# A GraphSAGE layer with batch norm on one core: second-stage loads behind the last gathers, four tiles kept for a late turn, sums before squares

## The chip, the cores and the metric

One core of a Trainium2 chip. The metric is the device time of one execution in microseconds. TensorE is PE in the profile, VectorE DVE, ScalarE ACT, GpSimd POOL and SyncE SP.

## The reference

`x` is 50000 x 512 float32. The edges are 12500 random pairs in both directions and a loop at each node, sorted by target (75000 in all). Cut to what matters:

```python
summed = segment_sum(x[src], dst, n)
cnt    = segment_sum(ones, dst, n)
aggr   = summed / maximum(cnt, 1.0)[:, None]
h      = aggr @ W_l.T + b_l + x @ W_r.T
mu     = mean(h, axis=0);  var = mean(square(h - mu), axis=0)
h_norm = (h - mu) * rsqrt(var + 1e-5) * gamma + beta
out    = layernorm(x + relu(h_norm), axis=-1)
```

## The kernel before, in words

**Stage one** makes `h` in HBM (`h_scratch`) and its column sums. It writes `h = x @ (W_l + W_r).T + (aggr - x) @ W_l.T`. The first product is made for all rows; the second is zero for a node whose only edge is its loop, so it is made only for the others, the "slots".

- *Products.* 78 groups of 640 rows (five tiles of 128) and a last one of 80 rows, 391 tiles. Each float32 operand is split in a high and a low part, and a tile is twelve matmuls into `pd` (`product`, L506, L524 to L526). SP loads `raw`, ScalarE rounds it to `x_hi` (`x_high`, L722), VectorE makes `x_lo` (`x_low`, L1042; four operations to a group, placed behind the group before's tile number 2). ScalarE copies `pd` to `h_out` (`copy_h`, L730), and behind a group's tiles 1 and 2 makes two `x_hi` pieces of the next group each. SP stores the group.
- *Slots.* 78 pairs of 128 slots. For a pair, VectorE makes one-hot tables and indices (`indices`, L1055), GpSimd gathers five blocks of rows (`gather`, L1356: `xe`, then `xn` and `xf` for both halves h), VectorE begins the difference (`begin`, L1074), TensorE adds the extras (`spread_extras`, L606), VectorE ends it (`difference`, `dd`), TensorE transposes it (L621), ScalarE rounds to `dT_hi`, VectorE makes `dT_lo`, and TensorE makes `correction(u, h)` (L632, twelve matmuls into the one bank `pz`). ScalarE scales it into `zz` (`copy_z`, L788), and GpSimd scatters it with addition into `h_scratch` (`add_z`, L1370).
- *Sums.* SP reads a finished group back into `hs` (`load_sums`, L384), VectorE adds it to `acc1` (`take_sums`, L1103), ScalarE squares it in place (`square`, L795), VectorE adds the squares to `acc2` (`take_squares`, L1111).

The order is written out by hand: eight groups run first, then 84 **turns** `u` from -2 to 81. Turn `u` holds pair `u` (0 to 77), the tiles that `tiles_by` (L297) gives it, and the sums of group `u - 3`. In turns 0 to 74 those are four or five tiles. Each engine has its own list of a turn's steps; on TensorE (L685 to L710):

```python
spread 0, tile 0, spread 1, tile 1, transposes 0, tile 2, transposes 1,
tile 3, correction 0, tile 4 (if there is one), fill_slots(u + 2), correction 1
```

ScalarE's list (L830 to L861) copies tiles 0 to 3 with `dT_hi` between them, then the extras of pair `u + 1`, then z of half 0, then tile 4 and three squares; z of half 1 comes first in the next turn. `correction(u, 1)` waits for `copy_z(u, 0)`, since both halves use `pz`. Where a turn's first tile, or the last of five in the turn before, is number 2 of its group, VectorE makes `x_lo` ahead of the squares and of `dT_lo`. GpSimd in turn `u` issues `add_z(u-1, 1)`, the gathers of pair `u + 1`, and `add_z(u, 0)`. On VectorE `take_squares(u-4)` stands ahead of `dT_lo`, `take_sums(u-3)` behind it.

Once the last group is stored, in turn 74, SP issues `load_early` (L405): `h` and `x` of groups 0 to 2 for stage two, ahead of that turn's `load_sums`.

**Stage two** starts when both sums are complete (`s_done`): TensorE sums over partitions, VectorE and ScalarE make the scale and shift (`s_bnr`), and then every group is scaled by GpSimd (L1402), shifted, cut at zero and added to `x` by VectorE, squared and normalised by ScalarE, in nine buffers of `hx`. SP stores group k and then loads `x` of k + 9 and `h` of k + 8 (L495 to L500). ScalarE normalises group k - 1 after the squares of group k.

## Time and profile before

| what | value |
|---|---|
| three runs | 2591.77, 2595.24 and 2596.50 us, median 2595.24 |
| profiled execution | 2596.68 us, span 2594.9 us |
| PE, PEld | 68%, 55% of the span |
| DVE, ACT, POOL | 75%, 57%, 56% |
| HBM | read 515.32 MB, written 246.22 MB |
| queue of SP | 617.84 MB, 62.1% of the 16 engines' span |
| queue of POOL (gathers, scatters) | 132.51 MB, 20.7% |
| chain that ended last | PE 33%, DMA 32%, issue 9%, DVE 9%, ACT 8%, POOL 7% |

The shares are means over stages with different limits. The slices of the page show it: PE is busy nine tenths in slices 2 to 28 (65 us each) and not at all from slice 30 on, where the DMA engines move 410 to 426 GB/s. Slice 29, in which stage one ends, is at 163 GB/s with PE at six tenths.

### The profile page before, as it was taken

The numbers are of one execution on the slowest core, as the hardware profiler recorded it, in microseconds if no ns is written. First come the engines' busy times: TensorE is split into PE (matmuls) and PEld (weight loads), VectorE is DVE, ScalarE is ACT, GpSimd is POOL, SyncE is SP. The second block draws the span as 40 slices with busy tenths as digits, with TensorE's granted clock in tenths as the row PEclk, the third lists the DMA queues.
The fourth block names the chain that finished last, engine by engine and source line by source line (L and its number), as shares of the span: only waits on it lengthen the run. The fifth ranks groups of instructions, "written<-read, shape, count | busy, mean of one in ns | idle before, by whom it ended". The sixth has DMA issues, their size and how long they took to land.

```text
span 2594.9 us, 29629 instructions
## 1 busy us (share of the span) xinstructions
PE 1757.6 (68%) x9404; PEld 1415.7 (55%) x9404; DVE 1956.6 (75%) x3451; ACT 1471.8 (57%) x2847; POOL 1456.2 (56%) x700
## 2 busy tenths in 40 slices
PE   7899999999999999999999999996400000000000
PEld 5778778878877887787778778874200000000000
DVE  6745878888877888888788888785688666666666
ACT  4333455545554554454445445542389988888887
POOL 5354555555555555555565555554196655555564
PEclk9999999999999999999999999997755555555555
DMA  5466878887888878888788878877599999999998
GB/s 184 139 211 206 260 250 266 277 253 246 257 263 255 258 246 259 258 255 264 234 262 271 255 243 253 280 240 247 163 410 426 426 426 426 426 412 414 421 421 344
DMA packets 125533, 752.89 MB, mean 290 GB/s; under 512 B 20809, under 2 KB 20809, under 8 KB 65726
## 3 DMA queue, kind: packets, MB, share of 16 engines
q1 hardware_dynamic: 70464, 617.84, 62.1%
q0 software_dynamic: 53664, 132.51, 20.7%
q8 instruction: 77, 1.26, 0.2%
q10 hardware_dynamic: 1246, 0.60, 0.1%
q14 instruction: 82, 0.67, 0.1%
HBM read 515.32 MB, written 246.22 MB: 293 GB/s over the span
## 4 chain that ended last, share of the span: by engine, by line
PE 33%; DMA 32%; issue 9%; DVE 9%; ACT 8%; POOL 7%; SPq 0%; POOLq 0%; ACTq 0%; DVEq 0%
DMA out<-hx 19%; PE pd L524 7%; PE pd L526 7%; PE pd L525 7%; DMA xn<-x,gi 5%; DMA xf<-x,gi 5%; PE pz L627 3%; PE pz L629 3%; PE pz L628 3%; ACT hx L881 3%; POOL xn L1331 2%; ACT hx L891 2%; DVE x_lo L1045 2%; POOL xf L1331 2%; DMA hs<-h_scratch 1%
## 5 line engine op out<-in xcount | busy, mean ns | idle before, releaser
L524 PE MATMUL pd<-wc_hi,x_hi 128*128 128x512 f32 x1564 | 628.8, 402 | 34.8 <-DVE wc_lo L922 17.3
L1379 POOL DMA_INDIRECT h_scratch<-zz,si x156 | 308.8, 1979 | 564.5 <-ACT zz L793 506.9
L735 ACT ACTIVATE h_out<-pd 128x512 f32<-128x512 f32 x391 | 233.6, 597 | 672.3 <-PE pd L526 652.1
L526 PE MATMUL pd<-wc_hi,x_lo 128*128 128x512 f32 x1564 | 614.6, 393 | 0.0
L525 PE MATMUL pd<-wc_lo,x_hi 128*128 128x512 f32 x1564 | 612.9, 392 | 0.0
L1402 POOL TENSOR_TENSOR hx<-hx,scale_b 128x2560 f32<-128x2560 f32 (+2 forms) x91 | 439.4, 4838 | 293.3 <-DMA hx<-h_scratch 251.8
L524 PEld LDWEIGHTS pd<-wc_hi,x_hi 128*128 128x128 f32 x1564 | 295.4, 189 | 98.5 <-issue 29.9
L526 PEld LDWEIGHTS pd<-wc_hi,x_lo 128*128 128x128 f32 x1564 | 295.2, 189 | 64.7
L525 PEld LDWEIGHTS pd<-wc_lo,x_hi 128*128 128x128 f32 x1564 | 295.9, 189 | 57.9
L1331 POOL DMA_INDIRECT xn<-x,gi x156 | 264.9, 1698 | 47.7 <-issue 47.7
L881 ACT ACTIVATE hx<-hx,nm 128x512 f32<-128x512 f32 x391 | 277.1, 710 | 2.8
L891 ACT ACTIVATE hx<-hx,nr,rs 128x512 f32<-128x512 f32 x385 | 278.6, 798 | 0.0
L627 PE MATMUL pz<-wl_hi,dT_hi 128*128 128x512 f32 x624 | 256.5, 411 | 28.9 <-ACT zz L793 20.3
L1331 POOL DMA_INDIRECT xf<-x,gi x156 | 248.7, 1594 | 47.6 <-issue 47.3
L1079 DVE SCALAR_TENSOR_TENSOR xf<-xn,ndeg,xf 128x512 f32<-128x512 f32 x156 | 114.9, 746 | 185.8 <-issue 140.3
L799 ACT ACTIVATE hs<-hs 128x512 f32<-128x512 f32 x391 | 219.1, 621 | 51.1 <-DVE acc L1109 51.1
L628 PE MATMUL pz<-wl_lo,dT_hi 128*128 128x512 f32 x624 | 247.4, 396 | 0.0
L629 PE MATMUL pz<-wl_hi,dT_lo 128*128 128x512 f32 x624 | 246.4, 395 | 0.0
L728 ACT ACTIVATE x_hi<-raw 128x640 fp32r<-128x640 f32 (+1 forms) x316 | 214.1, 724 | 40.7 <-DMA raw<-xT_whole 40.6
L1109 DVE TENSOR_TENSOR acc<-acc,hs 128x2560 f32<-128x2560 f32 (+1 forms) x79 | 220.1, 2786 | 21.7 <-DMA hs<-h_scratch 21.7
L1116 DVE TENSOR_TENSOR acc<-acc,hs 128x2560 f32<-128x2560 f32 (+1 forms) x79 | 220.2, 2787 | 16.0 <-ACT hs L799 16.0
L1045 DVE TENSOR_TENSOR x_lo<-raw,x_hi 128x640 fp32r<-128x640 f32 x280 | 209.4, 808 | 14.7 <-ACT x_hi L728 14.7
(221 smaller groups left out, 2855.0 us busy)
## 6 DMA issues: line engine op xcount, KB each, us to landing
raw<-xT_whole SPq DMA_DIRECT2D x78, 1280.0 KB
h_scratch<-h_out SPq DMA_DIRECT2D x78, 1280.0 KB
hs<-h_scratch SPq DMA_DIRECT2D x78, 1280.0 KB
hx<-x SPq DMA_DIRECT2D x78, 1280.0 KB, 20.7
hx<-h_scratch SPq DMA_DIRECT2D x77, 1280.0 KB, 15.4
out<-hx SPq DMA_DIRECT2D x77, 1280.0 KB, 18.0
xn<-x,gi POOLq DMA_INDIRECT x156
xf<-x,gi POOLq DMA_INDIRECT x156
```

The costliest lines, as they stand in the source:

```text
L524: pe.matmul(pd[i][0:n, :], hi, wc["hi"][:, kc, :], start=kc == 0, stop=False)
L525: pe.matmul(pd[i][0:n, :], hi, wc["lo"][:, kc, :], start=False, stop=False)
L526: last = pe.matmul(pd[i][0:n, :], lo, wc["hi"][:, kc, :], start=False, stop=kc == KC - 1)
L627: pe.matmul(out_bank[0:n, :], hi, wl["hi"][:, kc, :], start=kc == 0, stop=False)
L628: pe.matmul(out_bank[0:n, :], hi, wl["lo"][:, kc, :], start=False, stop=False)
L629: last = pe.matmul(out_bank[0:n, :], lo, wl["hi"][:, kc, :], start=False, stop=kc == KC - 1)
L881: act.activation(hb[i][0:n, t, :], xb[i][0:n, t, :], ACT.Square, bias=nm2[0:n, k % 4, t:t + 1], accum_out=ssq2[0:n, k % 4, t:t + 1]).then_ ...
L891: act.activation(hb[i][0:n, t, :], xb[i][0:n, t, :], ACT.Identity, bias=nr2[0:n, k % 4, t:t + 1], scale=rs2[0:n, k % 4, t:t + 1]).then_inc ...
L1045: dve.tensor_tensor(x_lo[:, b, kc, 0:n], raw[:, b, kc, 0:n], x_hi[:, b, kc, 0:n].bitcast(F32), ALU.subtract).then_inc(s_xld, 1)
L1331: return pool.indirect_dma_start(out=table if scatter else out, out_offset=by if scatter else None, in_=out if scatter else table, in_offs ...
L1379: pool.indirect_dma_start(out=h_dram[:, :], out_offset=by, in_=zz[:, h, :], in_offset=None, bounds_check=N + 2 * P - 1, oob_is_err=True, c ...
L1402: pool.tensor_tensor(hb[i][0:n, a:b], hb[i][0:n, a:b], scale_b[0:n].unsqueeze(1).to_broadcast([n, b - a, D]), ALU.mult).then_inc(s_mul, 1)
```

## The change

- `tiles_by`: four tiles (`HELD`) are kept back; turns 0 to 74 share the other 337, and turn 75 takes the four.
- TensorE, in a turn with fewer than five tiles: tile 3 moves from ahead of `correction(a, 0)` to behind it. ScalarE's order of steps is not changed.
- GpSimd: the gathers of pair `u + 1` come first in a turn, then `add_z(u-1, 1)` and `add_z(u, 0)`. `zz` has two copies by `u % 2`, with a semaphore for each; a scatter now waits itself for the one of the pair before.
- Behind the last pair (turns 78 and later) VectorE takes the sums of a group ahead of the squares of the one before. Groups 76 and 77 are read back into `h_out`.
- SP: two groups of stage two are loaded in turn 77, behind the load of group 75's sums and once all gathers have landed, four more (`KEPT` is 6) behind the last `load_sums`. The order of the places in `hx` is changed so that these don't touch `h_out`.
- Stage two: group 0 is normalised before the squares of group 1.

```diff
-            return min(len(later), TG * EARLY - (TG * EARLY - len(later)) * (u + 1) // (U - REACH))
+            if u >= U - REACH:
+                return len(later)
+            return TG * EARLY + (len(later) - HELD - TG * EARLY) * (u + 1) // (U - REACH)
...
+        def sums_of(g):
+            return h_out[:, g % 2] if isinstance(g, int) and G - 2 <= g < G else hs[:, g % 2]
...
-                if g >= 2:
-                    sp.wait_ge(s_a2, g - 1)
-                sp.dma_start(part_of(hs[:, b], g), group_of(h_dram, g)).then_inc(s_sl[b], 16)
+                if G - 2 <= g < G:
+                    sp.wait_ge(s_st[0], stored(G))
+                    sp.wait_ge(s_st[1], stored(G - 1))
+                elif g >= 2:
+                    sp.wait_ge(s_a2, g - 1 if g < G else G - 3)
+                sp.dma_start(part_of(sums_of(g), g), group_of(h_dram, g)).then_inc(read_back(g), 16)
...
-                        if g == G:
-                            load_early()
                     if sums_at(u + 1) is not None:
                         load_sums(sums_at(u + 1))
+                    if u == U - 1:
+                        sp.wait_ge(s_ge, 16 * U)
+                        for h in range(2):
+                            sp.wait_ge(s_gn[h], 16 * U)
+                            sp.wait_ge(s_gf[h], 16 * U)
+                        sp.wait_ge(s_dm, TG * G + 1)
+                        load2(0, EARLY2)
+                sp.wait_ge(s_z, 2 * U)
+                load2(EARLY2, KEPT)
...
-                    plain(3)
+                    if len(tiles) == TG:
+                        plain(3)
                     if a is not None:
                         correction(a, 0)
-                    plain(4)
+                    plain(3 if len(tiles) < TG else 4)
...
-                if u > 0:
-                    act.wait_ge(s_sc[h], 16 * u)
-                act.activation(zz[:, h, :], pz[:], ACT.Copy, scale=wgt[:, u % 4, h:h + 1]).then_inc(s_ze, 1)
+                if u > 1:
+                    act.wait_ge(s_sc[h][u % 2], 16 * (u // 2))
+                act.activation(zz[:, u % 2, h, :], pz[:], ACT.Copy, scale=wgt[:, u % 4, h:h + 1]).then_inc(s_ze, 1)
...
-                if k >= 1 and not by_vector(k - 1):
+                if k == 0:
+                    normalise(0)
+                if k >= 2 and not by_vector(k - 1):
                     normalise(k - 1)
...
-                    if sums_at(u - 1) is not None:
+                    if u < U and sums_at(u - 1) is not None:
                         take_squares(sums_at(u - 1))
...
                     if sums_at(u) is not None:
                         take_sums(sums_at(u))
+                    if u >= U:
+                        take_squares(sums_at(u - 1))
...
+                    if u > 0:
+                        pool.wait_ge(s_sc[h][(u - 1) % 2], 16 * ((u - 1) // 2) + 16)
...
                     p = pair_at(u)
+                    if pair_at(u + 1) is not None:
+                        gather(u + 1, 0)
+                        gather(u + 1, 1)
                     if pair_at(u - 1) is not None:
                         add_z(u - 1, 1)
-                    if pair_at(u + 1) is not None:
-                        gather(u + 1, 0)
-                    if pair_at(u + 1) is not None:
-                        gather(u + 1, 1)
                     if p is not None:
                         add_z(p, 0)
```

How it moves the instructions, at three places. On TensorE, in the last four-tile turn ahead of turn 74, from the transposes of half 1 on (`pd` is a tile's bank, `pz` a correction's); before:

```order
L621 MATMUL p<-ident,dd 128x128 x4
L524 MATMUL pd<-wc_hi,x_hi 128x512
L525 MATMUL pd<-wc_lo,x_hi 128x512
L526 MATMUL pd<-wc_hi,x_lo 128x512
L524 MATMUL pd<-wc_hi,x_hi 128x512
```

The same place in the changed kernel:

```order
L641 MATMUL p<-ident,dd 128x128 x4
L647 MATMUL pz<-wl_hi,dT_hi 128x512
L648 MATMUL pz<-wl_lo,dT_hi 128x512
L649 MATMUL pz<-wl_hi,dT_lo 128x512
L647 MATMUL pz<-wl_hi,dT_hi 128x512
```

The correction's twelve matmuls follow the transposes at once; the tile's twelve stand behind them. The end of that tile in the changed kernel, up to the second correction:

```order
L544 MATMUL pd<-wc_hi,x_hi 128x512
L545 MATMUL pd<-wc_lo,x_hi 128x512
L546 MATMUL pd<-wc_hi,x_lo 128x512
L620 MATMUL psl<-vals,hot 128x6 x13
L623 MATMUL psl<-valsx,hotx 128x4 x10
L647 MATMUL pz<-wl_hi,dT_hi 128x512
```

Only `fill_slots` (`psl`) is left between the tile and the second correction. On ScalarE, in the changed kernel's turn 75, from tile 2 on:

```order
L756 ACTIVATE h_out<-pd 128x512 [waits h_summed]
L807 ACTIVATE dT_hi<-p 128x512 [waits z_summed,differences_transposed]
L756 ACTIVATE h_out<-pd 80x512 [waits h_stored0,h_summed]
L801 ACTIVATE xe_hi<-xe 128x512 [waits extras_spread,extras_gathered]
L814 ACTIVATE zz<-pz,wgt 128x512 [waits z_added0_1,weights_ready,z_summed]
L820 ACTIVATE hs<-hs 128x512 [waits sums_taken]
```

The order is that of before: the copy of tile 3 (`h_out`), of the extras, of z. On SP, from the load of group 75's sums on, in the changed kernel:

```order
L411 DMA hs<-h_scratch 128x2560 [waits z_added1_1,z_added1_0,z_added0_0,squares_taken,z_added0_1,h_stored1]
L418 DMA hx<-h_scratch 128x2560 [waits rows_gathered1,neighbours_gathered1,neighbours_gathered0,h_summed,rows_gathered0,extras_gathered]
L422 DMA hx<-x 128x2560
L418 DMA hx<-h_scratch 128x2560
L422 DMA hx<-x 128x2560
L411 DMA h_out<-h_scratch 128x2560 [waits z_added1_1,z_added1_0,h_stored0,z_added0_1,h_stored1,z_added0_0] x2
```

Four loads of stage two stand between the sums of group 75 and those of groups 76 and 77, which wait for both last scatters and no more for squares.

## Rows read from the trace of the kernel before

**Rows 1.** Windows: start:end, us, busy of PE, PEld, DVE, ACT, POOL; clock, DMA share, GB/s

```profile
184.63:1772.90 1588.27, 1553.51 (x8523) 1258.74 (x8521) 1273.34 (x1842) 777.05 (x1346) 894.97 (x524) 1.00 0.81 253
1286.44:1305.77 19.33, 19.03 (x108) 15.61 (x107) 15.72 (x15) 9.32 (x17) 14.00 (x7) 1.00 0.65 183
1328.65:1350.25 21.60, 21.60 (x120) 17.79 (x119) 18.58 (x31) 10.96 (x19) 11.72 (x7) 1.00 0.82 256
1772.90:1807.80 34.90, 13.06 (x60) 9.40 (x59) 13.08 (x20) 5.03 (x9) 11.45 (x7) 0.68 0.93 354
1914.50:2564.30 649.80, 0.00 (x0) 0.00 (x0) 463.43 (x1295) 552.53 (x1233) 398.00 (x72) 0.50 1.00 418
```

**Rows 2.** Waits of PE in 170:1740: us in total, times, longest

```profile
PE pz L627 <- ACT zz L793: 14.2, 33, 1.5
```

**Rows 3.** Timelines of DVE and POOL: start us, us, what, idle before

```profile
1309.70 0.75 DVE L1079 SCALAR_TENSOR_TENSOR xf<-xn,ndeg,xf 128x512 f32<-128x512 f32 x1 [6.89 <-issue]
...
1312.00 1.08 POOL L1331 DMA_INDIRECT xe<-x,gi  x1 [2.92 <-DVE si L1069]
```

**Rows 4.** Timelines of SP, ACT and DVE in turn 75

```profile
1774.70 0.37 SPq L392 DMA_DIRECT2D hs<-h_scratch  x1
...
1789.90 0.63 ACT L780 ACTIVATE xe_hi<-xe 128x512 fp32r<-128x512 f32 x1 [9.91 <-DMA xe<-x,gi]
...
1804.04 2.83 DVE L1109 TENSOR_TENSOR acc<-acc,hs 128x2560 f32<-128x2560 f32 x1 [21.69 <-DMA hs<-h_scratch]
```

**Rows 5.** Timeline of PE in the turn that begins at 1707.70

```profile
1720.46 0.39 PE L627 MATMUL pz<-wl_hi,dT_hi 128*128 128x512 f32 x1
...
1723.18 0.48 PE L600 MATMUL psl<-vals,hot 125*128 125x6 bf16 x13
...
1724.32 0.47 PE L627 MATMUL pz<-wl_hi,dT_hi 128*128 128x512 f32 x1 [0.41 <-ACT zz L793]
```

**Rows 6.** Timeline of ACT in the same turn

```profile
1720.66 0.60 ACT L735 ACTIVATE h_out<-pd 128x512 f32<-128x512 f32 x1 [2.11 <-PE pd L526]
1721.72 1.37 ACT L728 ACTIVATE x_hi<-raw 128x640 fp32r<-128x640 f32 x2 [0.46 <-DMA raw<-xT_whole]
1722.99 0.61 ACT L780 ACTIVATE xe_hi<-xe 128x512 fp32r<-128x512 f32 x1
1723.51 0.67 ACT L793 ACTIVATE zz<-pz,wgt 128x512 f32<-128x512 f32 x1
```

**Rows 7.** Timelines of DVE and PE in the turn that begins at 1286.44

```profile
1291.50 3.02 DVE L1045 TENSOR_TENSOR x_lo<-raw,x_hi 128x640 fp32r<-128x640 f32 x4
...
1297.18 0.68 DVE L1100 TENSOR_TENSOR dT_lo<-px,dT_hi 128x512 fp32r<-128x512 f32 x1
...
1296.35 0.48 PE L524 MATMUL pd<-wc_hi,x_hi 128*128 128x512 f32 x1
```

**Rows 8.** Timeline of PE at three idle stretches

```profile
792.23 0.68 PE L627 MATMUL pz<-wl_hi,dT_hi 128*128 128x512 f32 x1 [1.50 <-ACT zz L793]
...
795.69 0.42 PE L629 MATMUL pz<-wl_hi,dT_lo 128*128 128x512 f32 x1
...
1025.82 0.47 PE L627 MATMUL pz<-wl_hi,dT_hi 128*128 128x512 f32 x1 [1.52 <-ACT zz L793]
...
1273.19 0.47 PE L524 MATMUL pd<-wc_hi,x_hi 128*128 128x512 f32 x1 [2.33 <-issue]
```

**Rows 9.** Timeline of ACT behind the last turn with a pair

```profile
1845.55 2.71 ACT L799 ACTIVATE hs<-hs 128x512 f32<-128x512 f32 x5 [5.63 <-DVE acc L1109]
```

**Rows 10.** Timelines of POOL and SP: pair 77's last scatter, load of group 76

```profile
1839.67 1.56 POOL L1379 DMA_INDIRECT h_scratch<-zz,si  x1 [2.28 <-ACT zz L793]
...
1844.44 0.33 SPq L392 DMA_DIRECT2D hs<-h_scratch  x1
```

**Rows 11.** Timeline of SP: first late load, second store

```profile
1869.83 0.34 SPq L399 DMA_DIRECT2D hx<-h_scratch  x1
...
1914.54 0.34 SPq L493 DMA_DIRECT2D out<-hx  x1
```

More of the change, by code:

```diff
@@ L32 @@
 LAG = 3
+HELD = 4
 EMPTY = 1 << 16
@@ L205, in bass_sage_batchnorm_residual_layernorm_kernel @@
         dd = sr("dd", [P, 2, D], F32)
-        zz = sr("zz", [P, 2, D], F32)
+        zz = sr("zz", [P, 2, 2, D], F32)
         spread = sr("spread", [P, PW], F32R)
@@ L214, in bass_sage_batchnorm_residual_layernorm_kernel @@
         s2 = allocator(ctx)
-        KEPT = 3
+        EARLY2, KEPT = 2, 6
         hx = s2("hx", [P, NB2, 2, TG, D], F32)
-        hb = [hx[:, i, 0] for i in range(NB2)]
-        xb = [hx[:, i, 1] for i in range(NB2)]
+        places = (0, 1, 3, 4, 5, 6, 2, 7, 8)
+        hb = [hx[:, i, 0] for i in places]
+        xb = [hx[:, i, 1] for i in places]
         bn = [hb[NB2 - 1][:, i, :] for i in range(5)]
@@ L263, in bass_sage_batchnorm_residual_layernorm_kernel @@
             "z_summed", "z_copied"))
-        s_sc = [sem(f"z_added{h}") for h in range(2)]
+        s_sc = [[sem(f"z_added{h}_{b}") for b in range(2)] for h in range(2)]
         s_sl = [sem(f"h_loaded{b}") for b in range(2)]
+        s_sl_end = [sem(f"h_end_loaded{i}") for i in range(3)]
         s_a1, s_sq, s_a2 = sem("sums_taken"), sem("squares_ready"), sem("squares_taken")
@@ L313, in pair_at, with read_back @@
             return u if 0 <= u < U else None
+        def sums_of(g):
+            return h_out[:, g % 2] if isinstance(g, int) and G - 2 <= g < G else hs[:, g % 2]
+        def read_back(g):
+            return s_sl_end[g - G + 2] if isinstance(g, int) and g >= G - 2 else s_sl[g % 2]
         def sums_at(u):
@@ L388, in load_sums @@
                 for h in range(2):
-                    sp.wait_ge(s_sc[h], 16 * (last + 1))
-                if g >= 2:
-                    sp.wait_ge(s_a2, g - 1)
-                sp.dma_start(part_of(hs[:, b], g), group_of(h_dram, g)).then_inc(s_sl[b], 16)
+                    for v in (last - 1, last):
+                        sp.wait_ge(s_sc[h][v % 2], 16 * (v // 2) + 16)
+                if G - 2 <= g < G:
[4 more added lines that the diff above has]
+                sp.dma_start(part_of(sums_of(g), g), group_of(h_dram, g)).then_inc(read_back(g), 16)
             def load2_h(k):
@@ L403, in load2_x, with load2 @@
                 sp.dma_start(part_of(xb[i], k), group_of(x, k)).then_inc(s_x2[i], 16)
-            def load_early():
-                sp.wait_ge(s_dm, TG * G + 1)
-                sp.wait_ge(s_ev, TG * G + 1)
-                sp.wait_ge(s_st[0], stored(G))
-                sp.wait_ge(s_st[1], stored(G - 1))
-                for k in range(KEPT):
+            def load2(first, end):
+                for k in range(first, end):
                     load2_h(k)
@@ L466, in _ @@
                 correct(G)
-                load_early()
+                sp.wait_ge(s_done, 1)
+                load2(0, KEPT)
             with sp.Else():
@@ L472, in _ @@
                             after_group(g, g % 2)
-                        if g == G:
-                            load_early()
                     if sums_at(u + 1) is not None:
                         load_sums(sums_at(u + 1))
+                    if u == U - 1:
[7 more added lines that the diff above has]
+                load2(EARLY2, KEPT)
             sp.wait_ge(s_done, 1)
-            for k in range(KEPT, NB2 - 1):
-                load2_h(k)
-                load2_x(k)
+            load2(KEPT, NB2 - 1)
             sp.wait_ge(s_bnr, 1)
-            load2_h(NB2 - 1)
-            load2_x(NB2 - 1)
+            load2(NB2 - 1, NB2)
             def store2(k):
@@ L1059, in indices @@
                     for h in range(2):
-                        dve.wait_ge(s_sc[h], 16 * (u - 3))
+                        dve.wait_ge(s_sc[h][u % 2], 16 * (u // 2) - 16)
                 dve.wait_ge(s_slot, u + 1)
@@ L1108, in take_sums @@
                     dve.wait_ge(s_a1, g)
-                dve.tensor_tensor(acc1[0:n, 0:t], acc1[0:n, 0:t], hs[0:n, g % 2, 0:t], ALU.add).then_inc(s_a1, 1)
+                dve.tensor_tensor(acc1[0:n, 0:t], acc1[0:n, 0:t], sums_of(g)[0:n, 0:t], ALU.add).then_inc(s_a1, 1)
             def take_squares(g):
@@ L1115, in take_squares @@
                     dve.wait_ge(s_a2, g)
-                dve.tensor_tensor(acc2[0:n, 0:t], acc2[0:n, 0:t], hs[0:n, g % 2, 0:t], ALU.add).then_inc(s_a2, 1)
+                dve.tensor_tensor(acc2[0:n, 0:t], acc2[0:n, 0:t], sums_of(g)[0:n, 0:t], ALU.add).then_inc(s_a2, 1)
             dve.wait_ge(s_flag, 1)
@@ L1275, in _ @@
                     sum_y(k, t)
-                if k >= 1:
+                if k == 0:
+                    invert(0)
+                if k >= 2:
                     invert(k - 1)
```

8 lines of the change are left out of this document (4 added, 4 removed).

## The prediction

> **What bounds the kernel now.** I read the stage windows first. The span has three parts [rows 1]. Up to 1772.9 us come turns 0 to 74: TensorE is busy 1553.5 of 1588.3 us at full clock, so it sets their pace, and whatever makes it wait there is paid in full. A turn runs from one `pe` matmul to the next; an undisturbed turn with four tiles takes 19.33 us, one with five 21.60 us. From 1914.5 to 2564.3 us TensorE does nothing and the DMA engines move 418 GB/s at a share of 1.00: the second stage is bound by transfers. In the passage between them neither is full. What the passage gains moves the end one for one. What the turns lose does too, and there are 75 of them.
>
> The list of who waited for whom gives TensorE's largest wait in the turns: 14.2 us for the copy of z, in 33 turns [rows 2]. That looks like little to gain or lose. But by the split of the tiles turns 0 to 74 have 34 turns of four and 41 of five; 34 x 19.33 + 41 x 21.60 = 1542.8, so 45.5 us of the 1588.3 lie above the undisturbed lengths. The timelines of VectorE and GpSimd show where they come from: in a disturbed turn VectorE sits idle 6.89 us before it can use the last gather, the indices follow, and the next gathers start only 6.2 us into the turn that began at 1305.77 [rows 3]. So VectorE begins the next turn late, and TensorE waits for its results.
>
> **The change, part by part.**
>
> *1. Four tiles kept.* Turns 0 to 75 now hold 39 turns of four tiles and 37 of five. Undisturbed: 39 x 19.33 + 37 x 21.60 = 1553.1 us. Before, turns 0 to 74 and turn 75, which held no tile but lasted 34.9 us [rows 1], took 1623.2 us. Turn 75 was that long because six second-stage loads stood in SP's queue ahead of the sums of group 72: these were issued at 1774.70, VectorE sat idle 21.69 us for them, and ScalarE waited 9.91 us for the extras' gather [rows 4]. With the loads gone to turn 77, turn 75 is a plain four-tile turn. So parts 1 and 2 together could give 1623.2 - 1553.1 = 70.1 us.
>
> *2. Gathers ahead of the last scatter.* The five gathers no longer stand behind a scatter and behind what that waits for; they wait for the indices alone. I take 37 of the 45.5 us as gained and 8 as left (bounds: 45.5 and 0). z twice, and the scatter's new wait for the one before it, I cost at nothing: the rows show no wait of ScalarE for a scatter, and a scatter has a whole turn to land. The scatter moved behind the gathers delays the load of sums by some 8 us; its reader comes a turn later. On GpSimd five gathers take about 9 of 21 us and hide there.
>
> *3. The fourth tile of a four-tile turn goes behind the first correction.* This is what costs, in two waits.
>
> First, the second correction needs the bank that ScalarE empties with `copy_z(u, 0)`, and ScalarE's order is the old one: copy of tile four, copy of the extras, then z. Tile four now comes after the first correction, so z waits for tile four. In the turn that began at 1707.70 the copy of tile four starts 0.20 us after TensorE has issued that tile (1720.66 against 1720.46). The extras' copy follows in about 0.5 us (copies of this size start 0.52 us apart, 1722.99 and 1723.51), z in 0.52 us more, and TensorE goes on 0.81 us after z's start, at 1724.32 [rows 5, 6]. That makes 2.04 us from the tile's end; the old order needed 1.14 us from the correction's end at 1723.18, `fill_slots` included. The idle of 0.41 us becomes 1.3 us: 0.90 us more. In 16 of the 39 turns tile four is number 1 or 2 of its group, and two `x_hi` copies (1721.72 to 1722.99, 1.27 us) stand between: 2.17 us more, an idle of 2.6. Together 23 x 0.90 + 16 x 2.17 = 55.4 us.
>
> Second, the first correction now follows the transposes at once and needs `dT_lo(0)`. In 15 of these turns four `x_lo` operations stand ahead of the squares and `dT_lo`. In such a turn, with VectorE on time, the first `dT_lo` ended at 1297.86, while TensorE had left the transposes at 1296.35 [rows 7]: 1.5 us, hidden so far by tile four (2.72 us, as a correction of twelve matmuls too, 1720.46 to 1723.18). That is 22.5 us. Without `x_lo` there `dT_lo` is 2.9 us earlier and in time. But the last of the 16 stalls and the first of these do not add exactly, and I take 71 us for the two waits, between 60 and 78.
>
> *4. The clock.* An idle stretch costs more than itself when the granted clock falls. After 1.50 us at 792.23 the next eight matmuls took 3.46 us, 0.43 each and not 0.23, which is the lower of the two levels: 1.6 us lost. So it was after 2.33 us at 1273.19; after 1.52 us at 1025.82 it was not [rows 8]. I let the 16 stalls of 2.6 us all pay (26 us), the 23 of 1.3 us once in three (12 us), the `dT_lo` stalls once in five (5 us): 43 us. Bounds: 0, and all 54 x 1.6 = 86 us.
>
> *5. The end of stage one.* The chain of turns 76 and 77 stays. Behind it the last groups were summed at one in 8.34 us, since squares waited for sums and sums for squares (2.71 us of squares, 5.63 us of waiting) [rows 9]. Sums first hides the squares and would save 2.7 us a group, 8 us. What is late next is the load of group 76, now into the free `h_out`: it needs pair 77's last scatter, issued at 1839.67, that is 31.9 us into turn 76, and landed by 1844.44 in a quiet queue [rows 10]. TensorE enters turn 76 warm, so I put the issue at 29.5 us; 4.8 us to land, some 5 us of load (1.31 MB at 418 GB/s and a start), and six sums and squares (15 us) behind it end at 54.5 us, against 62 before (1807.8 to 1869.83 [rows 11]). But now four loads of 1.31 MB run beside that scatter. The nearest row is the gather that ScalarE waited 9.91 us for beside six loads; with it the end is at 60. I take 57: 5 us gained, between 2 and 8.
>
> A rule speaks for the upper end here and against part 1. The Trainium skill, "DMA: Bandwidth & Descriptors", section on queues, rings and completion order, has each DMA engine alternate between its queues packet by packet. By it the scatter would pass the loads and the sum would be 2 to 3 us lower; nor would the early loads have held up the extras' gather, where the row with 9.91 us does not agree.
>
> *6. Second stage.* Before, its second store came at 1914.54, 44.7 us after the first late load [rows 11], with the queue just run dry. Six groups loaded early empty the queue sooner, but the second store still waits for VectorE and ScalarE: only the first comes earlier, and load 9 of h stands behind the second in SP's order. Then 649.8 us bound by transfers as before. I take 1 us; bounds 0 and 3.
>
> **The sum.** Turns 0 to 75: 1553.1 + 71 + 43 + 8 = 1675 against 1623.2: +52. End -5, second stage -1: +46 on the profiled execution's own 2596.7 us (its span is 2594.9, and it lies 1.4 us over the runs' median 2595.2): **2643 us**, 1.8% slower.
>
> **The rivals.**
>
> *Faster: the stalls stay under the break-even.* Four-tile turns may lose (70.1 - 8 + 6) / 39 = 1.75 us each before the change loses; with the clock steady they lose 1.82. With the clock steady, all 45.5 us gained, the end at -8 and the second stage at -3, the result is 2596.7 - 70.1 + 71 - 11 = 2587. For it: 1.52 us of idle once left the clock up. Against it: 2.33 us did not, and 16 turns get a longer one. Chance 0.10.
>
> *The gathers do not cure VectorE's lateness.* If traffic and not the late issue sets their landing, the 37 us stay, and a late VectorE also delays `dT_lo` in the four-tile turns, where tile four no longer hides it, by at least 0.4 us in 39: 2643 + 37 + 15 = 2695. For it: a DMA share of 0.81 in the turns [rows 1]. Against: the issue is late in the rows. Chance 0.13.
>
> *The reordering does nothing*, because TensorE had slack: 2596.7 - 70.1 + 8 - 6 = 2529. It is busy 98% of the turns. Chance 0.04.
>
> **Chances.** The forecast's mechanism with its spread (2605 to 2680) has 0.65, the same with few falls of the clock (2590 to 2605) 0.08, of which 0.05 within 0.2% (5 us, about what a measurement of this kernel can tell from no change). Faster 0.14, same 0.05, slower 0.81. The range 2595 to 2695 leaves out the faster cases and half of the uncured one.
>
> **What the profile would show.** Right: four-tile turns of 20.2 to 23 us; TensorE's wait for the z copy at 55 to 80 us; a wait for `dT_lo` of some 20 us that was next to nothing; half-clock stretches in the turns; five-tile turns near 21.6; turn 75 near 21; the last sums back to back. Wrong: four-tile turns at 19 us (the stall is not there), five-tile turns still at 23 (the gathers), or a second stage that is shorter from the first late load on.

## The result, and the profile after

The changed kernel takes **2653.7 us**, median of 4 runs (2644.8 to 2658.4), against 2595.9 for the kernel before beside it (2591.8 to 2598.6): a ratio of 1.022, with a 95% interval of 1.020 to 1.0241. The forecast was 2643 us, slower. The profiled execution took 2650.5 us (span 2648.5). Its stage windows have the columns of [rows 1]:

```profile
184.66:1836.78 1652.12, 1564.15 (x8475) 1278.78 (x8472) 1271.69 (x1846) 768.62 (x1340) 849.34 (x524) 0.98 0.79 244
1836.78:1857.19 20.41, 19.11 (x109) 15.14 (x107) 15.17 (x25) 8.06 (x16) 12.16 (x7) 1.00 0.56 162
1953.00:1966.00 13.00, 0.00 (x0) 0.00 (x0) 11.49 (x30) 9.33 (x26) 13.00 (x4) 0.50 0.57 239
1966.00:2618.00 652.00, 0.00 (x0) 0.00 (x0) 465.84 (x1303) 555.41 (x1237) 400.63 (x72) 0.50 1.00 416
```

The first row is turns 0 to 74: 1652.1 us and not 1588.3, with the mean clock at 0.98 and not 1.00. The second is turn 75, 20.4 us and not 34.9. Turns 0 to 75 together take 1672.5 us against 1623.2: **49.4 us more**. The last row is the second stage, bound by transfers as before; the one above it shows its queue running dry for some us once the groups loaded early are used up. From the start of turn 76 to the first late load (SP's timeline, below) it is 65.7 us against 62.0: **3.7 us more**. From there to the second store 45.5 against 44.7, from there to the end 680.1 against 680.4: half a us. The sum, 53.6 us, is the difference of the spans (2648.5 - 2594.9).

Where the turns lose it stands in TensorE's waits in turns 0 to 75 (us in total, times, longest):

```profile
PE pz L647 <- ACT zz L814: 70.7, 39, 2.6
PE pz L647 <- DVE dT_lo L1123: 18.5, 14, 1.4
```

The wait for z was 14.2 us [rows 2], the one for `dT_lo` 1.4 us. The list has no other row: the small waits for gathers and differences are gone. And 37 turns of five tiles took 802.6 us, 21.69 each, while 39 turns of four took 869.9, 22.31 each: a four-tile turn now takes longer than a five-tile one.

The clock shows in TensorE's timeline, here two turns with the same idle stretch:

```profile
793.30 0.47 PE L647 MATMUL pz<-wl_hi,dT_hi 128*128 128x512 f32 x1 [1.30 <-ACT zz L814]
793.61 0.40 PE L648 MATMUL pz<-wl_lo,dT_hi 128*128 128x512 f32 x1
...
795.91 0.39 PE L649 MATMUL pz<-wl_hi,dT_lo 128*128 128x512 f32 x1
...
1053.95 0.47 PE L647 MATMUL pz<-wl_hi,dT_hi 128*128 128x512 f32 x1 [1.30 <-ACT zz L814]
1054.26 0.47 PE L648 MATMUL pz<-wl_lo,dT_hi 128*128 128x512 f32 x1
...
1054.95 0.63 PE L647 MATMUL pz<-wl_hi,dT_hi 128*128 128x512 f32 x1
1055.38 0.63 PE L648 MATMUL pz<-wl_lo,dT_hi 128*128 128x512 f32 x1
...
1058.13 0.40 PE L649 MATMUL pz<-wl_hi,dT_lo 128*128 128x512 f32 x1
```

From the first to the last matmul of the correction it is 2.61 us in the first turn and 4.18 in the second, where seven matmuls follow each other 0.43 us apart and not 0.23, the lower of the two clock levels: 1.6 us lost behind one and the same 1.30 us of idle. In 23 of the 39 four-tile turns five or more steps are that long. Where they are only five the fall costs 1.2 us.

The end of stage one, from the timelines of GpSimd, SP and VectorE:

```profile
1888.02 1.55 POOL L1408 DMA_INDIRECT h_scratch<-zz,si  x1 [1.61 <-ACT zz L814]
...
1900.02 0.89 SPq L411 DMA_DIRECT2D h_out<-h_scratch  x2
...
1907.71 2.83 DVE L1132 TENSOR_TENSOR acc<-acc,h_out 128x2560 f32<-128x2560 f32 x1 [13.03 <-DMA h_out<-h_scratch]
1910.45 2.82 DVE L1139 TENSOR_TENSOR acc<-acc,hs 128x2560 f32<-128x2560 f32 x1
...
1922.94 0.33 SPq L418 DMA_DIRECT2D hx<-h_scratch  x1
```

Pair 77's last scatter is issued at 1888.02, 30.8 us into turn 76, and the load that waits for it can start only 12.0 us later; before it was 4.8 [rows 10]. VectorE's sums and squares then stand back to back.

### The profile page after: what moved, and what is told of

It is laid out like the page before. It is cut to its first block, busy times and chain, and to the rows that moved or that the text cites. A ratio compares the mean times of both kernels' runs of the same rounds, so it can differ in the third digit from the quotient of the medians.

```text
span 2648.5 us, 29863 instructions
## 1 busy us (share of the span) xinstructions
PE 1771.7 (67%) x9404; PEld 1439.2 (54%) x9404; DVE 1954.4 (74%) x3451; ACT 1465.7 (55%) x2847; POOL 1414.2 (53%) x700
## 4 chain that ended last, share of the span: by engine, by line
PE 58%; DMA 22%; ACT 8%; DVE 7%; issue 2%; POOL 2%; SPq 0%; ACTq 0%; DVEq 0%; POOLq 0%
DMA out<-hx 19%; PE pd L544 11%; PE pd L546 11%; PE pd L545 11%; PE pz L647 6%; PE pz L649 6%; PE pz L648 6%; ACT hx L902 3%; ACT hx L912 2%; DVE acc L1139 1%; DVE x_lo L1068 1%; PE px L641 1%; PE p L641 1%; DVE hot L1074 1%; DMA h_scratch<-zz,si 1%
## 5 line engine op out<-in xcount | busy, mean ns | idle before, releaser
L1408 POOL DMA_INDIRECT h_scratch<-zz,si x156 | 294.1, 1886 | 573.0 <-DVE xe_lo L1107 394.7
L544 PEld LDWEIGHTS pd<-wc_hi,x_hi 128*128 128x128 f32 x1564 | 295.3, 189 | 87.0 <-issue 17.7
L647 PE MATMUL pz<-wl_hi,dT_hi 128*128 128x512 f32 x624 | 269.6, 432 | 96.6 <-ACT zz L814 72.5
L546 PEld LDWEIGHTS pd<-wc_hi,x_lo 128*128 128x128 f32 x1564 | 294.2, 188 | 65.1 <-issue 0.5
L1358 POOL DMA_INDIRECT xn<-x,gi x156 | 288.2, 1847 | 47.7 <-issue 45.3
L649 PE MATMUL pz<-wl_hi,dT_lo 128*128 128x512 f32 x624 | 258.9, 415 | 0.0
L648 PE MATMUL pz<-wl_lo,dT_hi 128*128 128x512 f32 x624 | 258.1, 414 | 0.0
L1358 POOL DMA_INDIRECT xf<-x,gi x156 | 219.2, 1405 | 47.5 <-issue 44.8
L1132 DVE TENSOR_TENSOR acc<-acc,hs 128x2560 f32<-128x2560 f32 (+1 forms) x77 | 214.6, 2787 | 9.4 <-DMA hs<-h_scratch 9.4
L1139 DVE TENSOR_TENSOR acc<-acc,hs 128x2560 f32<-128x2560 f32 (+1 forms) x77 | 214.6, 2787 | 0.1
L814 ACT ACTIVATE zz<-pz,wgt 128x512 f32<-128x512 f32 x156 | 106.9, 685 | 170.0 <-PE pz L649 170.0
```

Source lines behind the costliest of these rows:

```text
L544: pe.matmul(pd[i][0:n, :], hi, wc["hi"][:, kc, :], start=kc == 0, stop=False)
L546: last = pe.matmul(pd[i][0:n, :], lo, wc["hi"][:, kc, :], start=False, stop=kc == KC - 1)
L647: pe.matmul(out_bank[0:n, :], hi, wl["hi"][:, kc, :], start=kc == 0, stop=False)
L648: pe.matmul(out_bank[0:n, :], hi, wl["lo"][:, kc, :], start=False, stop=False)
L649: last = pe.matmul(out_bank[0:n, :], lo, wl["hi"][:, kc, :], start=False, stop=kc == KC - 1)
L1139: dve.tensor_tensor(acc2[0:n, 0:t], acc2[0:n, 0:t], sums_of(g)[0:n, 0:t], ALU.add).then_inc(s_a2, 1)
```

## The experiments

Twelve kernels ran, in four groups beside the kernel before (medians there 2592.5, 2593.1, 2592.8 and 2593.1 us). The last two columns are from one profiled execution of each kernel: turns 0 to 75 are from one `pe` matmul to another in TensorE's timeline; the end is from turn 76 to the first late load.

| kernel | median us | ratio to before (95%) | turns 0-75 | end |
|---|---|---|---|---|
| before | 2595.9 | | 1623.2 | 62.0 |
| changed | 2653.7 | 1.022 (1.020-1.024) | 1672.5 | 65.7 |
| e1 tile at its old place | 2561.5 | 0.988 (0.984-0.992) | 1580.1 | 65.9 |
| e2 z copied first | 2541.9 | 0.981 (0.978-0.984) | 1565.3 | 64.9 |
| e3 idle filled | 2611.4 | 1.007 (1.005-1.010) | 1635.6 | 65.1 |
| e4 = e1, loads behind sums | 2550.2 | 0.983 (0.980-0.986) | 1579.9 | 55.2 |
| e5 = e4, gathers behind | 2577.2 | 0.993 (0.991-0.995) | 1612.0 | 60.0 |
| e6 = e4, both orders | 2532.3 | 0.977 (0.975-0.978) | 1560.7 | 57.4 |
| e7 = e4, z once | 2554.1 | 0.985 (0.982-0.988) | 1576.4 | 56.0 |
| e8 = e4, squares first | 2550.8 | 0.984 (0.982-0.987) | 1574.4 | 61.6 |
| e9 = e4, no tile kept | 2557.4 | 0.987 (0.984-0.989) | 1585.0 | 55.8 |
| e10 = e6, extras first | 2523.3 | 0.973 (0.971-0.975) | 1552.7 | 58.8 |
| e11 = e9, four loads in turn 75 | 2569.1 | 0.991 (0.988-0.993) | 1596.6 | 58.8 |
| e12 = before, tile's new place alone | 2713.9 | 1.044 (1.038-1.050) | 1744.4 (0-74: 1712.2, before 1588.3) | 62.0 |

**e1: the fourth tile back in front of the first correction.**

```diff
-                    if len(tiles) == TG:
-                        plain(3)
+                    plain(3)
                     if a is not None:
                         correction(a, 0)
-                    plain(3 if len(tiles) < TG else 4)
+                    plain(4)
```

> The changed kernel, with the fourth tile of a four-tile turn back in front of the first correction; everything else of the change stays. Theory (the tile's new place is what costs; the other parts gain what they were priced at): four-tile turns return to 19.33 us, five-tile turns stay at 21.6, so turns 0 to 75 take 39 x 19.33 + 37 x 21.60 = 1553 us and some 3 more, against 1672.5: about 116 us less than the changed kernel, 2537 us (2530 to 2550), faster than both kernels. Rival 1 (the loss sits in the gathers and the scatter's new place, or in DMA traffic): the time stays within 20 us of 2654. Rival 2 (the shorter turns bring VectorE's lateness back, since a gather then has 2.5 us less to land): five-tile turns of 22 to 23 us and 2555 to 2575.

92 us of turns came back, and the kernel is 1.2% faster than before: rival 1 falls, the tile's place is what costs. But the time is 24 us above the 2537 expected. The four-tile turns took 778.2 us and not 754. Most are at 19.35; 21 of the 24 us sit in eight of them, one in each ten turns, in which TensorE waits up to 2.9 us for z; 13 us are the longer waits, and in five of the eight the clock falls behind them (8 us). The timelines of ScalarE and TensorE in one of them:

```profile
1717.70 1.36 ACT L748 ACTIVATE x_hi<-raw 128x640 fp32r<-128x640 f32 x2 [1.71 <-DMA raw<-xT_whole]
1719.49 0.67 ACT L813 ACTIVATE zz<-pz,wgt 128x512 f32<-128x512 f32 x1
...
1720.31 0.71 PE L647 MATMUL pz<-wl_hi,dT_hi 128*128 128x512 f32 x1 [1.65 <-ACT zz L813]
```

ScalarE copies `x_hi` ahead of z, and in the shorter turns the load of x transposed comes late for that copy. Rival 2 had the right amount and the wrong place.

**e2: the new order kept, ScalarE copies z first in four-tile turns.**

```diff
-                    plain(tiles[3:4])
+                    if len(tiles) == TG or a is None:
+                        plain(tiles[3:4])
...
                         copy_z(a, 0)
+                        if len(tiles) < TG:
+                            plain(tiles[3:4])
```

> The changed kernel with TensorE's new order kept; in four-tile turns ScalarE copies z(0) ahead of the fourth tile and of the extras. Theory (the stall is ScalarE's unchanged order, not TensorE's new one): TensorE's wait for the z copy goes from 70.7 us to under 20, and the 15 waits for dT_lo of about 1.3 us stay. 39 x 18.92 + 37 x 21.60 + 15 x 1.3 + some 5 us of clock = 1562 against 1672.5: about 110 us less, 2543 us (2530 to 2560). Rival (any idle time behind the first correction is set by the way through the bank itself: GpSimd or VectorE is late then, or the x_hi copies that now end 0.5 us later hold up the next turn's first matmuls by as much as was gained): 2600 us or more, with a new wait of TensorE for x_hi or for the fourth tile's bank.

2541.9 us against 2543 expected. TensorE's two rows of waits for the correction, over the whole execution (14 of those for `dT_lo`, 19.0 us, lie in turns 0 to 75):

```profile
PE pz L647 <- DVE dT_lo L1126: 24.5, 16, 2.8
PE pz L647 <- ACT zz L814: 1.7, 2, 0.9
```

Without x_lo ahead of it a four-tile turn now takes 18.88 us (19.46 in seven), less than the 19.33 of the old order; with x_lo ahead 20.5, which is 1.2 more. The 39 four-tile turns take 763.7 us, against 870.0 in the changed kernel and 778.2 in e1. So TensorE's new order costs only where x_lo stands ahead, through `dT_lo`; what made it dear is that ScalarE's list was left as it was. In none of the 39 turns does the clock fall.

**e3: dummy matmuls in the idle stretch.** They go into the bank of the extras, and their product is read by nobody.

```diff
+                    if a is not None and len(tiles) == 4:
+                        g3, t3 = tiles[3]
+                        for i in range(8 if t3 in (1, 2) and g3 < G else 4):
+                            pe.matmul(pe_[:], wl["hi"][:, 0, 0:P], wl["hi"][:, 0, :], start=True, stop=True)
```

> The changed kernel plus dummy matmuls of 128 columns behind fill_slots in every four-tile turn of stage one (4, or 8 where the fourth tile is number 1 or 2 of its group), into the bank of the extras; their product is read by nobody. Theory (a stall costs itself and, in some 24 turns, 1.6 us more because the granted clock falls): the fillers lie inside the stall, which shrinks by their own length and ends at the same moment, so only the clock's part comes back: 24 x 1.6 = 38 us at most, 2616 to 2630 us, and four-tile turns near 20.3 plain and 21.5 with x_hi. Rival (the slow matmuls behind a stall have another cause than idle time, or the fillers come out longer than the stall): 2650 or more.

The time fell by 42 us to 2611.4 by the medians, a little below the range expected, and by 35.5 us between the profiled executions. Not one of the 39 four-tile turns holds a half-clock step, and the turns are 36.9 us shorter (34.1 of them in the four-tile turns), against at most 23 x 1.6 = 37 for the falls counted. The timeline of TensorE in one of them:

```profile
782.05 1.16 PE L733 MATMUL pe<-wl_hi 128*128 128x512 f32 x4
783.50 0.47 PE L647 MATMUL pz<-wl_hi,dT_hi 128*128 128x512 f32 x1 [0.28 <-ACT zz L818]
```

Four fillers leave 0.28 us of the idle; the turn stays at 20.36 us, as without them when the clock held. They do no useful work and cost nothing. With the clock up throughout, the kernel is still 0.7% slower than the one before.

**e4: e1, with the first loads of the second stage behind the last loads of the sums.**

```diff
-                        load2(0, EARLY2)
                 sp.wait_ge(s_z, 2 * U)
-                load2(EARLY2, KEPT)
+                load2(0, KEPT)
```

> As the first of these runs (fourth tile in its old place), and besides the first four loads of the second stage are issued behind the last loads of the sums and not ahead of the last scatter. Theory (the last scatter took 12.0 us because four loads of 1.31 MB ran beside it, and the sums of the last two groups wait for it): it lands 4.8 us after its start, the first late load comes some 7 us earlier counted from the start of turn 76 (about 58.5 us and not 65.7), and since the second stage's first stores still come after its queue has been filled, the time is 5 to 8 us below the first run. Rival (the second stage needs the early start of its loads; its first groups then are late by what the loads lost, some 16 us less of reading ahead): within 2 us of the first run or slower.

11 us below e1 by the medians, 8.4 by the spans (2548.1 against 2556.5) with turns of the same length; 5 to 8 were expected. The timelines of GpSimd, SP and VectorE, first in e1:

```profile
1797.02 1.55 POOL L1407 DMA_INDIRECT h_scratch<-zz,si  x1 [4.39 <-ACT zz L813]
...
1807.27 0.89 SPq L411 DMA_DIRECT2D h_out<-h_scratch  x2
...
1816.42 2.82 DVE L1131 TENSOR_TENSOR acc<-acc,h_out 128x2560 f32<-128x2560 f32 x1 [11.43 <-DMA h_out<-h_scratch]
```

The same in e4:

```profile
1795.32 1.55 POOL L1406 DMA_INDIRECT h_scratch<-zz,si  x1 [1.61 <-ACT zz L812]
...
1800.20 0.89 SPq L411 DMA_DIRECT2D h_out<-h_scratch  x2
...
1805.58 2.83 DVE L1130 TENSOR_TENSOR acc<-acc,h_out 128x2560 f32<-128x2560 f32 x1 [3.23 <-DMA h_out<-h_scratch]
...
1820.81 0.38 SPq L418 DMA_DIRECT2D hx<-h_scratch  x1
```

Without the four loads the load that waits for the scatter starts 4.9 us after the scatter's issue, against 10.3 in e1 and 12.0 in the changed kernel, and takes 5.4 us itself, against 9.2 and 7.7. The end is 10.7 us shorter; from the first late load on, the second stage takes 2.4 us more than in e1 (727.3 against 724.9 to the end of the span), having read ahead less.

**e5: e4, with the gathers again behind the last scatter.**

```diff
+                    if pair_at(u - 1) is not None:
+                        add_z(u - 1, 1)
                     if pair_at(u + 1) is not None:
                         gather(u + 1, 0)
                         gather(u + 1, 1)
-                    if pair_at(u - 1) is not None:
-                        add_z(u - 1, 1)
```

> As the kernel with the fourth tile in its old place and the loads behind the sums (2550.2 us, turns 0 to 75 in 1579.9 us), with one thing more undone: the next pair's five gathers again behind the last scatter of the pair before. Theory (the late issue of the gathers is what made VectorE late before, and the new place cures it): VectorE is late again in the disturbed turns, first difference 2.8 us and more into the turn and not 0.65, five-tile turns of 22 to 26 us, turns 0 to 75 longer by 30 to 45 us, 2580 to 2595 us. Rival (traffic, not the issue, sets the landing, and the cure came with something else): within 8 us of 2550.

27 us more, a little below the range expected. In the profiled execution the turns are 32 us longer, but it is the slowest of the five, 10.8 us above their median. VectorE's waits have the gathers back at the top:

```profile
DVE xf L1100 <- issue: 141.1, 55, 8.0
DVE xf L1100 <- DMA xf<-x,gi: 39.6, 16, 5.4
```

In e4 these two rows read 9.0 and 5.3 us. The place of the gathers is worth 27 us in this order of the tiles by the medians, up to 32 in one execution.

**e6: e4, with the new order in the 24 four-tile turns where no x_lo stands ahead of `dT_lo`, the old one in the other 15, and z ahead of the `x_hi` copies in both.**

```diff
+                    late = a is not None and len(tiles) < TG and not behind_lows(u)
+                    if not late:
+                        plain(3)
...
+                    plain(3 if late else 4)
...
+                    if four and behind_lows(u):
+                        copy_h(tiles[3][0], tiles[3][0] % 2, tiles[3][1])
+                        copy_z(a, 0)
+                        highs(tiles[3:4])
+                    elif four:
+                        copy_z(a, 0)
+                        plain(tiles[3:4])
```

> Loads behind the sums, and in the 24 four-tile turns in which no x_lo stands ahead of dT_lo the changed kernel's order (fourth tile behind the first correction) with ScalarE copying z(0) ahead of that tile's copy; in the other 15 the old order, with z(0) copied ahead of the x_hi and extras copies. Theory (each of the two waits is the fault of one order in one kind of turn, and so neither is left): 24 x 18.88 + 15 x 19.35 + 37 x 21.67 + some 4 us = 1549 against 1579.9, so 2519 us (2512 to 2530), the fastest so far, with TensorE's waits for z and dT_lo both under 12 us in the turns. Rival (the shorter turns hand the wait on: gathers, the loads of x, or ScalarE's later x_hi copies become what TensorE waits for): 2535 us or more, with a new row in TensorE's list of waits.

2532.3 us: neither. The four-tile turns are near what was worked out (751.8 us, against 743.4), but the five-tile turns rose to 808.9 us: 15 of the 37 take 22.0 to 22.2 us and not 21.6. The edit had put the extras' copy behind z and the fourth tile's copies, and VectorE, which works on it, came late. The row in its list of waits is the first below; the second is the same one in e10.

```profile
DVE xe_lo L1124 <- ACT xe_hi L805: 71.1, 32, 4.6
```

```profile
DVE xe_lo L1123 <- ACT xe_hi L805: 10.7, 5, 5.5
```

**e7: e4, with one buffer for z.**

```diff
-                if u > 1:
-                    act.wait_ge(s_sc[h][u % 2], 16 * (u // 2))
-                act.activation(zz[:, u % 2, h, :], pz[:], ACT.Copy, scale=wgt[:, u % 4, h:h + 1]).then_inc(s_ze, 1)
+                if u > 0:
+                    act.wait_ge(s_sc[h][(u - 1) % 2], 16 * ((u - 1) // 2) + 16)
+                act.activation(zz[:, 0, h, :], pz[:], ACT.Copy, scale=wgt[:, u % 4, h:h + 1]).then_inc(s_ze, 1)
```

> As the kernel with the fourth tile in its old place and the loads behind the sums (2550.2 us), with one buffer for z as before the change: ScalarE's copy of z waits for the scatter of the pair before. Theory (as priced: nothing, since a scatter has the best part of a turn to land): within 4 us of 2550, no wait of ScalarE for a scatter over 0.5 us in the list. Rival (with the gathers in front the second scatter is issued some 9 us into the next turn and takes up to 10 us to land, so that the copy of z waits for it and TensorE behind it): 10 to 60 us more.

4 us more by the median, within the runs' spread (2547.8 to 2556.8 beside 2546.6 to 2551.0), and 2.8 us less by the span. ScalarE did wait for scatters, which the theory had denied:

```profile
ACT zz L812 <- DMA h_scratch<-zz,si: 10.3, 5, 3.2
```

Those waits did not reach TensorE: the four of them ahead of turn 76 fall in turns of 21.60, 21.60, 19.35 and 19.33 us, the undisturbed lengths. The second buffer has no effect here that this can tell.

**e8: e4, squares in front of the next sums at the end.**

```diff
-                    if u < U and sums_at(u - 1) is not None:
+                    if sums_at(u - 1) is not None:
                         take_squares(sums_at(u - 1))
...
-                    if u >= U:
-                        take_squares(sums_at(u - 1))
```

> As the kernel with the fourth tile in its old place and the loads behind the sums (2550.2 us), with the squares of the last groups again in front of the next group's sums. Theory (squares behind sums hide ScalarE's squaring, 2.7 us a group): the last sums end some 5 to 8 us later, the first late load too, 2555 to 2559 us. Rival (the end is set by the landing of the last scatter and load alone): within 2 us.

No difference in the medians, and so not the 2555 to 2559 us expected, but the profiles tell two things apart. VectorE waits again for ScalarE's squares,

```profile
1808.62 2.83 DVE L1137 TENSOR_TENSOR acc<-acc,h_out 128x2560 f32<-128x2560 f32 x1 [2.77 <-ACT h_out L818]
```

and the end is 6.5 us longer than in e4, within the 5 to 8 expected. In this execution the turns were 5.5 us shorter, for no reason in the edit. So the order of sums and squares is worth 6.5 us at the first late load; that the kernel's time moves with it is not shown.

**e9: e4, with `HELD = 0`.**

> As the kernel with the fourth tile in its old place and the loads behind the sums (2550.2 us), with no tile kept for turn 75: turns 0 to 74 hold 34 turns of four tiles and 41 of five as before the change, turn 75 none. Theory (of the 70 us that parts 1 and 2 had to give, the loads' new place and the gathers bring nearly all; an empty turn 75 lasts 13.8 us, as turn 76 does): 34 x 19.95 + 41 x 21.67 + 13.8 = 1580.6 against 1579.9 with four tiles kept, so within 5 us of 2550. Rival (the empty turn is no shorter than its chain of waits, or the last group stored earlier takes transfers from the sums): 8 to 20 us more.

7.2 us more, 5.1 in the turns: turn 75, empty, lasts 17.7 us and not 13.8. That lies between the two expectations, within 5 us and 8 to 20. Keeping four tiles for it brings 5 to 7 us.

**e10: e6, with the extras' copy ahead of z and of `x_hi`.**

```diff
                     if four and behind_lows(u):
                         copy_h(tiles[3][0], tiles[3][0] % 2, tiles[3][1])
-                        copy_z(a, 0)
-                        highs(tiles[3:4])
-                    elif four:
-                        copy_z(a, 0)
-                        plain(tiles[3:4])
...
                         extras_high(u + 1)
-                    if a is not None and not four:
+                    if a is not None:
                         copy_z(a, 0)
+                    if four and behind_lows(u):
+                        highs(tiles[3:4])
+                    elif four:
+                        plain(tiles[3:4])
```

> As the kernel with both orders (2532.3 us, turns 0 to 75 in 1560.7 us), with ScalarE's copy of the extras ahead of z(0) and of the x_hi copies in every four-tile turn. Theory (the 12 us missing there were VectorE's: its wait for the extras' copy rose to 71 us in 32 turns, from 16 in 7 where that copy goes first, and five-tile turns rose to 22.15): 24 x 18.9 + 7 x 0.57 + 15 x 19.35 + 37 x 21.67 = 1550, so 2521 us (2516 to 2527), VectorE's wait for the extras' copy under 25 us. Rival (x transposed is loaded too late for shorter turns, and VectorE waits for that): within 4 us of 2532.

2523.3 us, as expected: turns 1552.7 us, with 802.4 for the five-tile ones. VectorE's wait for the extras' copy, the second row under e6, is down to 10.7 us. This is the fastest kernel of the study, 2.7% below the kernel before and, by the medians, 4.9% below the changed one.

**e11: e9, with four loads of the second stage back in turn 75.**

```diff
                         if t == tiles_in(g) - 1:
                             after_group(g, g % 2)
+                        if g == G:
+                            sp.wait_ge(s_dm, TG * G + 1)
+                            sp.wait_ge(s_ev, TG * G + 1)
+                            sp.wait_ge(s_st[0], stored(G))
+                            sp.wait_ge(s_st[1], stored(G - 1))
+                            load2(0, EARLY2)
```

> As the kernel with no tile kept, with four loads of the second stage (1.31 MB each) issued at their place before the change, behind the last group's store in turn 75 and ahead of the sums of group 72. Theory (these loads, six of them before, made turn 75 34.9 us long, through VectorE's wait of 21.7 us for the sums of group 72): turn 75 takes 25 to 32 us in place of 13.8 and the time is 10 to 20 us above the kernel with no tile kept. Rival (the long turn came from the gathers' place, and is cured by it): within 4 us of the kernel with no tile kept.

11.8 us more than e9, turn 75 at 28.9 us, and the wait of before [rows 4] is back with its length for four loads and not six:

```profile
1778.41 2.83 DVE L1136 TENSOR_TENSOR acc<-acc,hs 128x2560 f32<-128x2560 f32 x1 [15.98 <-DMA hs<-h_scratch]
```

**e12: the kernel before, with the tile's new place alone** (the edit of e1, reversed).

> The kernel before the change, with one thing of the change alone: the fourth tile of a four-tile turn behind the first correction. Theory (the tile's place costs what undoing it gave back, 92.5 us of turns over 39 four-tile turns, so 2.37 us in each): 34 x 2.37 = 81 us more than before, 2675 us (2660 to 2690), TensorE's wait for z 50 to 65 us. Rival 1 (VectorE's lateness, which is still there, overlaps the new stalls, and the longer turns give the gathers the time they lacked): 35 to 60 us more, with fewer late turns. Rival 2 (the two add up and more, since a late VectorE delays dT_lo in turns where the fourth tile no longer hides it): 90 us more or above, with the wait for dT_lo over 30 us.

120.8 us more, well past the 81 of the theory. TensorE's waits up to 1900 us:

```profile
PE pz L627 <- ACT zz L794: 61.7, 34, 2.6
PE pz L627 <- DVE dT_lo L1101: 53.2, 20, 4.3
```

The wait for z is what 34 turns should have. The wait for `dT_lo` is nearly three times that of the changed kernel, in 20 turns: rival 2. With the gathers at their old place VectorE is late, and the tile that used to cover this is gone. Four-tile turns of 25 to 30 us stand beside others of 20.35. But rival 1's mechanism is there too. The 34 four-tile turns took 824.4 us against 666.6, 157.8 us more, while the 41 five-tile turns took 887.8 against 921.7, 33.9 less: none is over 22.1 us, though the gathers stand where they did, and in the kernel before the longest took 26.4. So the longer four-tile turns take the lateness out of the five-tile ones by themselves.

## Why the prediction was right

The sign, the size and the main mechanism held, and one step failed, the end of stage one; the range (2595 to 2695) was wider than the mechanism needed.

- **Four tiles kept, and the loads out of turn 75.** Turn 75 was to be a plain four-tile turn and is (20.4 us). Which part brings that the forecast did not separate. e9 and e11 do: the loads' place is worth 11.8 us for four loads, the four tiles 5 to 7.
- **The gathers.** 8 us of lateness were left over in the sum; the five-tile turns lie 3.4 us above 37 x 21.60. That alone does not show that the gathers cured them, since in e12 they are as short with the gathers behind. e5 shows it for the old order of the tiles, with 27 us by the medians and 32 in its slowest execution, of the 37 forecast; and between the kernel before and e9, which share the split of the tiles in turns 0 to 74, the five-tile turns differ by 34.8 us (921.7 against 886.9). The four-tile turns gave 13.8 us of that back (680.4 against 666.6), through the late loads of x transposed that e1 shows, which the forecast had not seen.
- **The two waits.** Forecast 71 us over what was there. Measured 70.7 + 18.5, less the 39 x 0.41 us of wait that the forecast gave the old order: 73.2. (Most four-tile turns of e1 wait 0.30 us there; with that it is 77.5.) The idle stretches of z were 1.30 and 2.55 us, forecast 1.3 and 2.6; the 14 of `dT_lo` 1.32, forecast 15 of 1.5.
- **The clock.** Forecast 43 us, by shares that were a guess from three rows. Measured 23 falls of up to 1.6 us, at most 37 us, and e3 gives 36.9 us back in the turns. Of the 16 stalls of 2.55 us 13 paid, where the forecast had all; of the 23 of 1.3 us ten, where it had a third; of the 14 for `dT_lo` none, where it had one in five. That the sum came out near is in part luck.
- **The turns** were to lose 52 us and lost 49.4.
- **The end of stage one is the step that failed.** The forecast was 5 us gained, between 2 and 8; it lost 3.7 us. The chain was right in all but two terms: issue at 30.8 us and not 29.5, sums and squares 15.2 and not 15. The scatter took 12.0 us where I had put 4.8, with 9.91 as the bound, and the load of group 76 took 7.7 and not 5 (in e1, with the same four loads, 10.3 and 9.2). I had taken a row from beside other loads as the worst case, and had charged the traffic to the scatter and not to the load behind it. e4 takes the loads away and gives 29.7 + 4.9 + 5.4 + 15.2 = 55.2 us, the forecast's sum for a quiet queue within 1 us (it says 54.5; its terms add up to 54.3).
- **The rule of the Trainium skill** weighed there ("DMA: Bandwidth & Descriptors", queues, rings and completion order: each engine alternates between its queues by packet) would, as the prediction applied it, have the scatter pass the loads. It did not: 12.0 us with the loads and 4.9 without do not agree with that as an account of when a small transfer has landed. Nothing here shows how the engines shared the packets.
- **The second stage** was to gain 1 us and lost half a us. Its queue ran dry, as foreseen.
- **The rival that was faster** needed an unchanged clock and a loss under 1.75 us in a four-tile turn. e3 gave it the clock, and the kernel stayed 0.7% slower than the one before, with 2.1 us lost in each (835.9 us in 39, against 19.33 each). e2 and e10 show what it lacked: TensorE's new order, in all four-tile turns or in 24 of them, with ScalarE's list adapted wins 1.9 and 2.7% over the kernel before.

What the forecast had not seen is how the two large parts hang together. With the gathers in front the tile's place costs 92.5 us in 39 four-tile turns, 2.37 each; in the kernel before, with them behind, 123.9 us net in 34 turns, 3.64 each. The gathers' place is worth 27 to 32 us in the old order. In the new one it is worth more, by two estimates from e12: about 80 us with 39 x 1.27 us on top of 32, or 64 if the changed kernel's turns, at 22.31 and 21.69 us, are put in e12's split (1712.2 - 1647.8). One part of this change hid much of what another cost.

Open is why equal idle stretches sometimes lower the clock and sometimes do not. The length alone does not decide: one of 3.04 us in e9 left it up, the matmuls behind it 0.23 us apart.

```profile
976.97 0.47 PE L646 MATMUL pz<-wl_hi,dT_hi 128*128 128x512 f32 x1 [3.04 <-ACT zz L812]
...
978.88 0.39 PE L648 MATMUL pz<-wl_hi,dT_lo 128*128 128x512 f32 x1
979.11 0.39 PE L646 MATMUL pz<-wl_hi,dT_hi 128*128 128x512 f32 x1
```

It wasn't tried whether the stall could also be taken away by moving VectorE's x_lo.

## What to carry to other kernels

When a piece of work moves on one engine, write down next to it the order of every engine that serves it: here one step moved on TensorE put up to four copies of ScalarE (the tile's, two of `x_hi`, the extras') into a path that had been covered, and moving the z copy in ScalarE's list turned a loss of 2.2% into a gain of 1.9%. Price a stall together with what the clock adds behind it; for stalls of 1 to 3 us that was half as much again. And look at what runs beside the last small transfer of a stage: reading ahead that nobody waits for yet belongs behind it.

## What the hardware showed that was not expected

- An idle stretch of 1.30 us, behind the same matmuls of its turn, left the granted clock up at 793.30 and brought it down to the lower level at 1053.95. One of 2.55 us alone brought it down in 9 cases of 9; with a stretch of 1.32 us ahead of it in the same turn, in 4 of 7. The stretches ahead of the first correction, 1.32 to 1.35 us in 14 turns of the changed kernel and 1.32 to 1.68 in 14 of e2, brought it down in none.
- Dummy matmuls in an idle stretch kept the clock up in all 39 turns and bought 42 us of run time by the medians (e3).
- A scatter of 128 rows had landed 12.0 us after its issue (changed kernel) and 10.3 (e1) beside four loads of 1.31 MB, and 4.9 us without them (e4). The plain load behind it took 7.7, 9.2 and 5.4 us.
